# A graph layer by sorted one-hots on one core: the order of work at both ends of the sort loop, and six tiles moved from scatters to TensorE

## The reference

```python
messages = einsum('ei,oi->eo', x[dst], W) + b
out = segment_sum(messages * agg_weight, src, num_segments=100000)
y = x + out
m = mean(y, axis=-1, keepdims=True); v = var(y, axis=-1, keepdims=True)
result = (y - m) / sqrt(v + 1e-5)
```

## Time and profile before

| | us |
|---|---|
| median of 3 runs | 911.15 (911.13 to 911.59) |
| the profiled execution | 912.28 |
| its span | 910.6 |
| VectorE busy | 853.0 (94%) |
| TensorE busy | 718.8 (79%) |
| ScalarE busy | 650.4 (71%) |
| POOL busy | 604.1 (66%) |
| start of the first gather | 255.57 |

### The profile page before, as it was taken

One profiled execution on the slowest core, in us unless ns is written; L12 is line 12 of the kernel. 1 busy time (PEld: TensorE's weight loads), 2 busy tenths in 40 slices (PEclk: granted clock), 3 DMA queues, 4 the chain that ended last, 5 costly groups with the idle time before them and its releaser, 6 DMA issues.

```text
span 910.6 us, 24246 instructions
## 1 busy us (share of the span) xinstructions
PE 718.8 (79%) x7748; PEld 542.4 (60%) x7773; DVE 853.0 (94%) x3868; ACT 650.4 (71%) x1683; POOL 604.1 (66%) x608
## 2 busy tenths in 40 slices
PE   3869999999638877777778877787878778787784
PEld 2835555555326656666666666676667667676664
DVE  7978999999658999999999999999999999999997
ACT  0147777777504778788778877777777887877788
POOL 3047777776657777777777777677777777777710
PEclk9969999999857999999999999989899999989988
DMA  2001111110043766676666667666666667666653
GB/s 73 2 26 37 39 41 39 43 37 26 16 134 108 209 212 214 220 215 215 206 212 212 208 211 212 205 209 211 208 220 207 205 214 215 208 214 202 217 176 124
DMA packets 81228, 141.20 MB, mean 155 GB/s; under 512 B 19552, under 2 KB 20588, under 8 KB 81100
## 3 DMA queue, kind: packets, MB, share of 16 engines
q1 hardware_dynamic: 62476, 110.55, 36.7%
q0 software_dynamic: 18624, 29.08, 13.3%
HBM read 87.64 MB, written 51.93 MB: 153 GB/s over the span
## 4 chain that ended last, share of the span: by engine, by line
DVE 61%; issue 7%; POOL 4%; ACT 1%; PE 1%; DMA 0%; ACTq 0%; DVEq 0%; POOLq 0%
DVE stats L994 16%; DVE h L988 10%; DVE sel L979 10%; DVE rest L977 8%; DVE xl L982 7%; DVE mv L1000 7%; POOL xg L517 3%; DVE rstd L1004 1%; ACT y L1087 1%; POOL place_scratch L480 1%; DVE shift L1008 1%; DVE now L965 1%; DMA xg<-in_x,now 0%; PE bank L719 0%; ACT aggT L1074 0%
## 5 line engine op out<-in xcount | busy, mean ns | idle before, releaser
L517 POOL DMA_INDIRECT xg<-in_x,now x441 | 449.0, 1018 | 172.9 <-issue 129.4
L1087 ACT ACTIVATE y<-h,shift,rstd 128x128 f32<-128x128 f32 x784 | 320.1, 479 | 0.1
L719 PE MATMUL bank<-wT,aggT 128*128 128x128 f32 x1568 | 241.5, 300 | 0.0
L719 PEld LDWEIGHTS bank<-wT,aggT 128*128 128x128 f32 x1568 | 202.6, 202 | 28.2 <-issue 11.9
L689 PE MATMUL bank<-sel,xg 128*128 128x308 bf16 (+11 forms) x685 | 171.1, 262 | 23.6 <-DVE xl L982 23.5
L480 POOL DMA_INDIRECT place_scratch<-word_col,place_row x141 | 142.1, 1008 | 55.6 <-issue 50.6
L691 PE MATMUL bank<-sel,rest 128*128 128x308 bf16 (+11 forms) x685 | 177.2, 262 | 0.0
L994 DVE BATCH_NORM_STATS2 stats<-h 128x6 f32<-128x128 f32 x784 | 169.5, 278 | 0.2
L693 PE MATMUL bank<-sel,xl 128*128 128x308 bf16 (+11 forms) x685 | 167.4, 261 | 0.0
L1081 ACT ACTIVATE std<-mv,eps 128x4 f32<-128x4 f32 x196 | 58.3, 298 | 132.7 <-DVE mv L1000 132.6
L988 DVE SCALAR_TENSOR_TENSOR h<-bank,aw,xt 128x512 f32<-128x512 f32 x196 | 145.6, 743 | 0.8 <-PE bank L719 0.4
(11 more groups left out here) (154 smaller groups left out, 927.1 us busy)
## 6 DMA issues: line engine op xcount, KB each, us to landing
xt<-in_x SPq DMA_DIRECT2D x195, 256.0 KB, 3.7
out<-y SPq DMA_DIRECT2D x195, 256.0 KB, 2.4
xg<-in_x,now POOLq DMA_INDIRECT x441
hi_row<-hi_scratch SPq DMA_DIRECT2D x50, 128.0 KB
place_scratch<-word_col,place_row POOLq DMA_INDIRECT x141
place_scratch<-scattered SPq DMA_DIRECT2D x1, 441.0 KB, 3.5
scattered<-place_scratch SPq DMA_DIRECT2D x1, 441.0 KB, 3.2
src_rows<-in_src SPq DMA_DIRECT2D x1, 192.0 KB
```

The lines of the kernel that those rows point to most:

```text
L517: nc.gpsimd.indirect_dma_start(out=xg[:, m, k], out_offset=None, in_=x, in_offset=bass.IndirectOffsetOnAxis(ap=now[:, m, k, 0:1], axis=0)) ...
L719: last = nc.tensor.matmul(OUT[u % RO][:, nodes[j]], aggT[:, u % RO, nodes[j]], wT[:], start=False, stop=True, skip_group_check=True)
L1087: nc.scalar.activation(y[:, u, j], h[:, u, j], ACT.Identity, bias=shift[:, u, j:j + 1], scale=rstd[:, u, j:j + 1]).then_inc(s_y, 1)
```

## The change

- Of the last three blocks 10, 13 and 7 tiles were placed by TensorE; now it is 13, 16 and 7 (blocks 22, 23, 24). 256 tiles are placed and 135 scattered.
- The digits are computed from the permuted source number by one multiplication and two shifts, in fewer operations; the first digit is transposed and copied out while the second is computed. `hi_rows` comes after both and has a semaphore of its own.
- VectorE reads the totals and writes `excess` right behind the one-hots. The words, the other `turn` parts and small constants follow, then the scan, the first two rows of one-hots, the ratio, the origins; the three-way split of the bias comes last.
- TensorE transposes the words as each is ready; ScalarE copies them out ahead of `t_col`.
- ScalarE writes the zeros into `xg` as its first work (a copy of ones, scaled by 0); POOL's memset is gone.
- The overfull check of block 0 moves behind the block's slots.
- Behind the sort loop TensorE gets 64 matmuls of 128x512 whose results nobody reads.
- VectorE's `select` runs 4 groups ahead of `add_x` at first, 5 from group 4, 6 from group 8.

```diff
-    BY_PE = [10] * (B - 2) + [13, C - (B - 1) * BC]
+    BY_PE = [10] * (B - 3) + [13, BC, C - (B - 1) * BC]
...
+s_hi_rows = sem("s_hi_rows")
...
-    sp.wait_ge(s_rows, 1)
+    sp.wait_ge(s_hi_rows, 1)
...
-    sp.wait_ge(s_spill, 2)
+    sp.wait_ge(s_spill, 1)
...
-    nc.gpsimd.memset(xg[:], 0.0).then_inc(s_clean, 1)
-
...
-    pe.wait_ge(s_rows, 3)
+    pe.wait_ge(s_rows, 1)
...
+    pe.wait_ge(s_rows, 2)
...
-    pe.wait_ge(s_rows, 7)
+    pe.wait_ge(s_rows, 3)
+    turn_rows(bank[3], word1[:].bitcast(f32))
+    pe.wait_ge(s_rows, 4)
+    turn_rows(bank[2], word2[:].bitcast(f32))
...
-    turn_rows(bank[3], word1[:].bitcast(f32))
-    turn_rows(bank[2], word2[:].bitcast(f32))
+    pe.wait_ge(s_rows, 6)
...
+
+    pe.wait_ge(s_samec, 4 * B)
+    for _ in range(64):
+        nc.tensor.matmul(SAME[0][:], ident_bf[:], not_earlier[:].rearrange("p c e -> p (c e)"),
+                         start=True, stop=True, skip_group_check=True)
...
-    after(V.tensor_scalar(e1[:], src_rows[:], 2, P - 1, LSR, AND))
-    V.tensor_scalar(e2[:], src_rows[:], SPAN_N - GN, None, AND)
+    V.tensor_scalar(e1[:], src_rows[:], (1 << 18) - GN, None, AND)
+    after(V.tensor_scalar(e2[:], src_rows[:], 2, P - 1, LSR, AND))
...
-    after(V.tensor_tensor(e0[:], pos[:], e2[:], OR))
-    V.tensor_scalar(e2[:], src_rows[:], SPAN_BITS, None, LSR)
-    after(V.tensor_scalar(e0[:], e0[:], float(LISTS), None, ALU.mult))
-    V.tensor_scalar(e1[:], e0[:], SPAN_BITS, None, LSR)
-    after(V.tensor_scalar(e0[:], e0[:], SPAN_N - 1, None, AND))
-    after(V.scalar_tensor_tensor(chunk[:], e2[:], float(LISTS), e1[:], ALU.mult, ALU.add))
-    after(V.tensor_scalar(e0[:], e0[:], float(TAIL_FROM), None, ALU.is_ge))
-    after(V.scalar_tensor_tensor(bucket[:], chunk[:], 2.0, e0[:], ALU.mult, ALU.add))
-    V.tensor_scalar(e0[:], bucket[:], LO_BITS, None, LSR)
-    after(V.tensor_scalar(e1[:], bucket[:], LO - 1, None, AND))
-    V.tensor_copy(hi_rows[:], e0[:]).then_inc(s_rows, 1)
+    after(V.tensor_tensor(pos[:], pos[:], e2[:], OR))
+    after(V.tensor_scalar(bucket[:], pos[:], float(LISTS), None, ALU.mult))
+    after(V.tensor_scalar(e0[:], bucket[:], SPAN_BITS + LO_BITS - 1, None, LSR))
...
-    V.tensor_copy(turn[:, 2], e1[:]).then_inc(s_rows, 1)
-    V.tensor_copy(turn[:, 0], chunk[:]).then_inc(s_rows, 1)
+    V.tensor_scalar(e1[:], bucket[:], SPAN_N - 1, None, AND)
+    after(V.tensor_scalar(e2[:], bucket[:], SPAN_BITS, LO // 2 - 1, LSR, AND))
+    after(V.tensor_scalar(e1[:], e1[:], float(TAIL_FROM), None, ALU.is_ge))
+    V.scalar_tensor_tensor(turn[:, 2], e2[:], 2.0, e1[:], ALU.mult, ALU.add).then_inc(s_rows, 1)
+    V.tensor_copy(hi_rows[:], e0[:]).then_inc(s_hi_rows, 1)
+    dve.wait_ge(s_cols, 2)
+    V.tensor_copy(hi_col[:], bank[1][:]).then_inc(s_hilo, 1)
...
-    V.tensor_copy(hi_col[:], bank[1][:]).then_inc(s_hilo, 1)
...
+    def first_hots(k):
+        dve.wait_ge(s_hrow[k], 32)
+        V.tensor_scalar(oh_hiT[:, k], hi_row[:, k], part_half[:], None, ALU.is_equal).then_inc(s_hiT, 1)
+
...
-    after(V.tensor_scalar(e0[:], pos[:], 16, None, LSL))
-    V.tensor_scalar(word1[:], e2[:], FULL, None, OR)
-    V.tensor_scalar(e1[:], dst_rows[:], 15, 25, AND, LSL)
+    V.tensor_scalar(upper_half[:], part[:], 64.0, -64.0, ALU.is_ge, ALU.mult)
+    dve.wait_ge(s_hist, 1)
+    after(V.tensor_tensor(counts[:], SORT[0][0:HI, 0:LO], guard[:], ALU.add))
+    heads, tails = (counts[:].rearrange("h (c two) -> h c two", two=2)[:, :, i] for i in range(2))
+    V.scalar_tensor_tensor(excess[:], heads, -float(P), tails, ALU.add, ALU.add).then_inc(s_excess, 1)
+
+    V.tensor_scalar(word1[:], e2[:], FULL, None, OR).then_inc(s_rows, 1)
+    V.tensor_scalar(chunk[:], bucket[:], SPAN_BITS, None, LSR)
+    V.tensor_scalar(e0[:], pos[:], GN - 1, 16, AND, LSL)
+    after(V.tensor_scalar(e1[:], dst_rows[:], 15, 25, AND, LSL))
+    V.tensor_copy(turn[:, 0], chunk[:])
...
+    V.tensor_tensor(part_half[:], part[:], upper_half[:], ALU.add)
...
-    V.memset(spill_row[:, 0:1], 0.0).then_inc(s_spill, 1)
-
-    after(V.tensor_scalar(upper_half[:], part[:], 64.0, -64.0, ALU.is_ge, ALU.mult))
-    after(V.tensor_tensor(part_half[:], part[:], upper_half[:], ALU.add))
-
-    def first_hots(k):
-        dve.wait_ge(s_hrow[k], 32)
-        V.tensor_scalar(oh_hiT[:, k], hi_row[:, k], part_half[:], None, ALU.is_equal).then_inc(s_hiT, 1)
-
+    after(V.memset(spill_row[:, 0:1], 0.0))
+    dve.wait_ge(s_excess_row, 16)
+    V.tensor_tensor_scan(spill_row[:, 1:NS + 1], excess_row[:], zero_row[:], 0.0, ALU.add, ALU.max
+                         ).then_inc(s_spill, 1)
...
-
-    dve.wait_ge(s_hist, 1)
-    after(V.tensor_tensor(counts[:], SORT[0][0:HI, 0:LO], guard[:], ALU.add))
-    heads, tails = (counts[:].rearrange("h (c two) -> h c two", two=2)[:, :, i] for i in range(2))
-    V.scalar_tensor_tensor(excess[:], heads, -float(P), tails, ALU.add, ALU.add).then_inc(s_excess, 1)
+    early = 4 * BC
+    dve.wait_ge(s_cvt, 4)
+    after(V.reciprocal(ratio_col[:, 0:early], w1_col[:, 0:early]))
+    V.tensor_tensor(ratio_col[:, 0:early], w2_col[:, 0:early], ratio_col[:, 0:early], ALU.mult).then_inc(s_ratio, 1)
+    dve.wait_ge(s_spilled, 16)
+    origins = origin[0:HI].rearrange("h (c two) -> h c two", two=2)
+    V.tensor_copy(origins[:, :, 0], spilled[:]).then_inc(s_origin, 1)
+    V.tensor_tensor(origins[:, :, 1], spilled[:], heads, ALU.add).then_inc(s_origin, 1)
+    after(V.tensor_tensor(head_end[:], spilled[:], heads, ALU.add))
+    after(V.tensor_reduce(most_hi[:], head_end[:], AX, ALU.max))
+    V.tensor_scalar(most_wide[:], ones[0:HI], most_hi[:], None, ALU.mult).then_inc(s_mx, 1)
...
-    dve.wait_ge(s_excess_row, 16)
-    V.tensor_tensor_scan(spill_row[:, 1:NS + 1], excess_row[:], zero_row[:], 0.0, ALU.add, ALU.max
-                         ).then_inc(s_spill, 1)
-    dve.wait_ge(s_cvt, 6)
-    early = 4 * BC
-    after(V.reciprocal(ratio_col[:, 0:early], w1_col[:, 0:early]))
-    V.tensor_tensor(ratio_col[:, 0:early], w2_col[:, 0:early], ratio_col[:, 0:early], ALU.mult).then_inc(s_ratio, 1)
-    dve.wait_ge(s_spilled, 16)
-    origins = origin[0:HI].rearrange("h (c two) -> h c two", two=2)
-    V.tensor_copy(origins[:, :, 0], spilled[:]).then_inc(s_origin, 1)
-    V.tensor_tensor(origins[:, :, 1], spilled[:], heads, ALU.add).then_inc(s_origin, 1)
-    after(V.tensor_tensor(head_end[:], spilled[:], heads, ALU.add))
-    after(V.tensor_reduce(most_hi[:], head_end[:], AX, ALU.max))
-    V.tensor_scalar(most_wide[:], ones[0:HI], most_hi[:], None, ALU.mult).then_inc(s_mx, 1)
...
-        if k == 0:
-            dve.wait_ge(s_mxT, 1)
-            after(V.tensor_reduce(most_all[:], SORT[1][:, 0:HI], AX, ALU.max))
-            V.tensor_scalar(over[:], most_all[:], float(most), None, ALU.is_gt).then_inc(s_over, 1)
-            V.tensor_scalar(keep[:], most_all[:], float(most), None, ALU.is_le)
-            after(V.tensor_scalar(most_all[:], most_all[:], float(most), None, ALU.is_gt))
-            after(V.tensor_scalar(dump[:], dump[:], most_all[:], None, ALU.mult))
...
+        if k == 0:
+            dve.wait_ge(s_mxT, 1)
+            after(V.tensor_reduce(most_all[:], SORT[1][:, 0:HI], AX, ALU.max))
+            V.tensor_scalar(over[:], most_all[:], float(most), None, ALU.is_gt).then_inc(s_over, 1)
+            V.tensor_scalar(keep[:], most_all[:], float(most), None, ALU.is_le)
+            after(V.tensor_scalar(most_all[:], most_all[:], float(most), None, ALU.is_gt))
+            after(V.tensor_scalar(dump[:], dump[:], most_all[:], None, ALU.mult))
...
-        rounds([(fetch, 0), (add_x, 13), (select, 7), (moments, 13), (invert, 14), (combine, 13),
-                     (recentre, 14)])
+        def one(stage, g):
+            if 0 <= g < GA:
+                stage(g, g % R, g // R, g // SPAN_G, g // SPAN_G % RX, g // SPAN_G // RX)
+
+        lead = lambda g: min(6, 4 + g // 4)
+        for g in range(lead(0)):
+            one(select, g)
+        for g in range(GA + 1):
+            one(fetch, g + 13)
+            one(add_x, g)
+            for ahead in range(g + lead(g), g + 1 + lead(g + 1)):
+                one(select, ahead)
+            one(moments, g)
+            one(invert, g - 1)
+            one(combine, g)
+            one(recentre, g - 1)
...
+    act.wait_ge(s_made, 1)
+    nc.scalar.activation(xg[:].rearrange("p r k d -> p (r k) d"), ones[:].unsqueeze(1).broadcast_to([P, RX * LISTS, D]),
+                         ACT.Copy, scale=0.0).then_inc(s_clean, 1)
...
-    for turned_back, (column, turned) in enumerate(((t_col[:], bank[0]), (w1_col, bank[3]), (w2_col, bank[2]),
+    for turned_back, (column, turned) in enumerate(((w1_col, bank[3]), (w2_col, bank[2]), (t_col[:], bank[0]),
```

## The result

The changed kernel took 897.48 us (median of 4 runs, 896.28 to 900.4) against 911.37 us for the kernel before in the same session (4 runs, 911.13 to 912.7): a ratio of 0.9851, 95% interval 0.9828 to 0.9874. The forecast was 896.9, in a range of 893.5 to 901.9; the gain is 13.9 us where 14.25 was forecast. The profiled execution is the slowest of the four, 900.4 us, with a span of 898.2 against 910.6.

A forecast was written before the change was run, and what follows sets the result against it. VectorE was taken to bound the main loop, so the question was its earlier start and early starving. Front 6.7 + sort end 5.55 + gathers 2.0 = 14.25 us off 912.28 gave 898.0, median 896.9; range 893.5 to 901.9.

The forecast's parts named there:

- Front, up to the one-hots: VectorE's bucket digits at the start: shorter work puts the first one-hot at 13.3 instead of 16.90, 3.6 us earlier.
- Histogram to the carry: Totals read at 33.0, scan at 37.6, block 0's carry at 42.1 to 42.4 instead of 49.59, 7.3 us earlier.
- The hold by POOL's casts: Shared port before block 0: POOL's index casts could hold VectorE's origins until 42.3, carry at 42.4 instead of 42.1.
- Block 0's pace: TensorE's matmuls of block 0, at clock 0.50 before: full clock saves at most 0.8 us, half taken, 0.4.
- rival A: TensorE at half clock around its first groups, no clock gain in block 0, lead loses 1.0: 900.3 us; chance 0.20.
- Front: Everything up to block 0's first slots: 7.3 + 0.4 - 1.0 = 6.7 us gained, bounds 5.5 and 7.3.
- End of the sort: Wait ahead of the merge: six tiles moved to TensorE end the reload's wait, gain 5.55 us, bounds 4.8 and 6.2.
- Start of the gathers: First groups: smaller lead lets additions come sooner; 2.0 us taken, 2.0 to 3.3 at full clock, 1.0 lost at half.
- B: Front, sort end and gathers all reach their good bounds: 7.3 + 6.2 + 3.3 = 16.8 us, 894.3; chance 0.12.
- C: Scatters don't shift with the front because POOL is held; reload at 243.9 sets the merge: 901.4 us; chance 0.07.
- D: In front, the origins' 2.87 us were not POOL's zeroing and stay; carry at 43.5, 898.1 us; chance 0.07.
- E: Extra matmuls behind the sort run at half clock, 27.5 us, delaying group 0: slower, 915 us; chance 0.02.

The follow-up runs named there:

- after_again: The changed kernel run again with no edit, for a second trace: 898.33 us, ratio 0.9856 to the kernel before.
- lead_six: The changed kernel with select six groups ahead from the first group, as before the change: 897.5 us, ratio 0.9848 to the kernel before.
- no_fill: The changed kernel without the 64 extra matmuls behind the sort loop: 897.34 us, ratio 0.9854 to the kernel before.
- front_fill: The changed kernel plus twelve spare transposes in TensorE's gaps ahead of block 0, on a slower chip: 1250.66 us, ratio 0.9985 to the kernel before.
- tiles_back: The changed kernel with six tiles given back from TensorE to the scatters: 905.5 us, ratio 0.9929 to the kernel before.
- pool_later: The changed kernel with POOL's constants from iota_nb on held until both digits are written, on a slower chip: 1253.49 us, ratio 0.9999 to the kernel before.

## Why the prediction was right

**Front, up to the one-hots: right.** 13.3 forecast, 13.25 to 13.28 in eight traces from three chips, 14.81 in the profiled one of the changed kernel. The terms written out for it add up to 13.1 (11.3 + 1.1 + 0.7); the two tenths more are not accounted for, and from the second digit on `after_again` took 1.93 where they have 1.8. What the working lacked is the spread of this step: it took durations from one trace, and a landing 0.3 later costs 1.56.

**Histogram to the carry: right in mechanism, 0.3 to 0.6 off.** In `after_again` the counts are read at 33.01, the scan stands at 37.50 and the carry at 42.73; forecast 33.0, 37.6 and 42.1 to 42.4 (between the excess and the scan the working lists fourteen operations, the code has thirteen; their 4.3 holds). The last copy ended at 40.6, forecast 40.7, and the matmuls ahead of the carry took 2.15 (40.60 to 42.75 in `lead_six`) and not the 1.4 that the kernel before showed; at full pace they took 1.3 (`no_fill`, 40.59 to 41.86). The 1.4 was itself a figure at the full pace, and the step took it over as if the pace were given. TensorE is the late one there, as said. The hold by POOL's casts, taken beside the sum, did not come, since the origins went first (42.12, the cast 42.27); in `front_fill` it came and took 0.4.

**Block 0's pace: the term was mis-sized.** The sum gave 0.4, half of "at most 0.8", and only for the matmuls behind the carry. There the two paces differ by 0.7 (carry to own 3.93 in `no_fill`, 4.61 in `after_again`), so the 0.8 was sound. What it left out is 0.9 more ahead of the carry, 1.56 in all at the use of the counts and 1.4 once more at block 2. The kernel before had the full pace ahead of the carry (a 128x512 matmul at 44.15 took 0.38) and the half pace behind it (the pair at 51.20 took 1.01); both traces of the changed kernel had the half pace on both sides, as rival A says for the part behind. Own came 7.1 earlier in `after_again` (54.42 to 47.34; 6.9 of it the carry's, 49.59 to 42.73) and 5.5 in the first trace; the check behind the first slots then took 0.9 (first use of counts to the second 10.98, before 10.08), forecast 1.0. Front: 7.1 - 0.9 = 6.2 in `after_again`, 4.6 in the first trace, with 7.7 to be had at full pace (`no_fill`), and 6.3 where `tiles_back` shows it at the merge; forecast 6.7, bounds 5.5 and 7.3. The bounds were too narrow on both sides.

**End of the sort: right.** 6.0 by `tiles_back`, forecast 5.55, bound 6.2. From the merge to the first gather nothing changed (3.95 and 3.94). The extra matmuls began at 239.08 in `after_again`; the prediction's 239.5 is 239.3 by its own terms.

**Start of the gathers: right in size, by another course.** The rest behind the first gather is 2.0 shorter, forecast 2.0 to 3.3 at full clock and -1.0 at half. The first addition stands 16.1 us behind the first gather (261.27 less 245.18) and 21.1 before (276.69 less 255.57): 5.0 less, forecast about 4. The waits did not go but changed kind, 5.4 for gathers and 6.3 ahead of additions, 11.7 together for 13.1 before; forecast near 10. The clock did not hold either. After a pause of 2.89 us TensorE was back at the lower level just where group 3 and its projection ran. Timeline and windows (length, busy PE, PEld, DVE, ACT, POOL; granted clock, DMA, GB/s) of the changed kernel:

```profile
261.27 0.75 DVE L991 SCALAR_TENSOR_TENSOR h<-bank,aw,xt 128x512 f32<-128x512 f32 x1 [2.00 <-PE bank L726]
...
264.12 0.20 PE L696 MATMUL bank<-sel,xg 128*128 128x57 bf16 x1 [2.89 <-DVE xl L985]
```

```profile
264.00:266.00 2.00, 1.88 (x16) 1.30 (x18) 1.23 (x9) 0.08 (x1) 1.70 (x2) 0.61 0.22 57
266.00:268.00 2.00, 2.00 (x15) 1.71 (x11) 0.00 (x0) 1.84 (x3) 1.39 (x3) 0.54 0.12 33
```

The second addition waited 3.02 (268.35) and yet nothing was lost against the forecast. The step's alternative, all at full clock or all at half, was too coarse: groups 0 to 2 at full clock were enough. Its price for the half clock was wrong. `no_fill` has the smaller lead and a granted clock of 0.50 to 0.55 from 248 to 252 and of 0.50 from 256 to 264, and its rest is 654.5: 0.5 gained or nothing, where 1.0 was to be lost. The additions themselves stand there nearly as worked out for the half clock, 17.7 and 24.9 behind the first gather for 18.3 and 25.3 (how the working comes to 280.9 for the second it doesn't show; 274.7 + 4.7 is 279.4). So the step that failed is the one from the additions' place to the loss. That the term met its 2.0 although the clock did not hold is in part luck.

**Rivals.** A: 900.3 for the median, which came at 897.48 and 898.33. Block 0 had no better pace, as A says, but behind the first gather 2.0 was gained in both traces where A has 1.0 lost. That the profiled execution took 900.4 is no sign of A: A gives 901.4 for a profiled one, and the front's late landing is in it. B: none of its three good bounds together; `no_fill` shows the front's. C and D are refuted: the scatters do shift with the front (the last one from 246.23 to 239.88 with the same tiles, in `tiles_back`), the merge is released by TensorE, and the origins' first operation takes 0.17 with the zeroing gone, while the zeroing put back costs 3.0 elsewhere. E did not occur, 64 matmuls took 13.8 at full pace, group 0 stood at 254.85 and the third group's first operation at 256.92; its price was not measured.

**The sum.** For `after_again`: 6.2 + 6.1 + 2.0 = 14.3 of span, forecast 14.25 (6.1 is what the merge gained beyond the front, 12.34 - 6.2). For the first trace: 4.6 + 5.8 + 2.0 = 12.4. In the one the three terms each lie within 0.6 of their forecast; in the other the front is 2.1 short, 1.56 of it from the landing. The medians show less than the 14.3: 13.9 in the first session and 13.1 in that of `after_again` (911.46 to 898.33). The sum starts from a trace of the kernel before that took 1.13 us more than its median, and takes these 1.13 off again; the trace of `after_again`, at 898.2, lies on its median.

## What to carry to other kernels

Where a wait ends a stage, find which engine is next behind it and cost the shift up to there: six moved scatters freed 7.9 us, and 6.0 arrived. A long fill on POOL is best moved to an engine that is idle and doesn't hold VectorE (beside ScalarE's fill, 2.10 to 6.14, VectorE's operations took 0.42 to 0.43 in `pool_later`), since on POOL it can hold one operation of VectorE or another, not only the one where the trace happened to show it. A term read from one trace whose engine stood at one of two paces needs both prices in the range, and two small edits may be worth little or nothing alone (0.5 each at most) and more together (2.0), so undo them one at a time before keeping or dropping either. Where a gain is smaller than the runs' own spread, as this one is, milestones of a trace can point to it, but single traces don't prove it.
